# Edges in their own order, duplicates summed by an equality matrix, and sums kept in four DRAM tables

## The reference

```python
e = relu(edge_feat @ We1 + be1) @ We2 + be2          # 40000 x 256, hidden 512
msg = relu(node_feat[src] + e)
out_h = segment_sum(msg, dst, num_segments=2500)
out = relu(((1 + eps) * node_feat + out_h) @ Wn1 + bn1) @ Wn2 + bn2
```

## Time and profile before

| | us |
|---|---|
| median of 3 runs (3002.50 to 3002.54) | 3002.51 |
| span of the profiled execution | 3198.3 |
| TensorE busy in it | 2348.5 |
| VectorE busy | 1951.0 |
| POOL busy | 1194.9 |
| ScalarE busy | 1141.6 |

### The profile page before, as it was taken

The page is one execution under the profiler, slowest core; times in us unless marked ns, Lnnn a source line. Parts: engine busy times, 40 slices in busy tenths (PEclk is TensorE's granted clock), DMA queues, the critical chain, the costliest instruction groups (busy, mean ns, idle before and its releaser), DMA issues. The chain is left out here.

```text
span 3198.3 us, 54121 instructions
## 1 busy us (share of the span) xinstructions
PE 2348.5 (73%) x14408; PEld 1941.4 (61%) x14409; DVE 1951.0 (61%) x5493; ACT 1141.6 (36%) x2522; POOL 1194.9 (37%) x1158
## 2 busy tenths in 40 slices
PE   0994899999999999999743499997125556554676
PEld 0331788888888888888743388886124434443565
DVE  7997566666566666666683644444445555556773
ACT  0994334343343343434320155554011222212221
POOL 0001555555555555655000011111536676663000
PEclk9997899999999999999875699999567676766787
DMA  0001222222222222223100367675222233225000
GB/s 39 0 0 56 75 72 68 70 74 71 72 69 69 72 71 67 76 69 73 26 0 32 114 235 248 237 246 173 61 72 81 78 88 85 79 83 48 19 8 32
DMA packets 129241, 256.68 MB, mean 80 GB/s; under 512 B 26393, under 2 KB 64326, under 8 KB 128563
## 3 DMA queue, kind: packets, MB, share of 16 engines
q0 software_dynamic: 56480, 145.84, 17.1%
q1 hardware_dynamic: 72708, 110.19, 10.1%
HBM read 238.57 MB, written 17.34 MB: 80 GB/s over the span
## 5 line engine op out<-in xcount | busy, mean ns | idle before, releaser
L455 POOL DMA_INDIRECT edge_ea<-in_edge_attr_dram,edge_edge_idx x332 | 339.8, 1023 | 611.7 <-DVE edge_edge_idx L615 520.8
L578 ACT ACTIVATE edge_whole<-edge_h_ps,edge_b 128x512 f32<-128x512 f32 x332 | 227.3, 685 | 655.5 <-PE edge_h_ps L374 385.1
L1594 POOL DMA_INDIRECT att_got<-head_table,att_idx x352 | 372.0, 1057 | 225.3 <-issue 115.4
L461 POOL DMA_INDIRECT edge_nf<-node_table,edge_node_idx x332 | 359.4, 1082 | 221.0 <-DVE edge_node_idx L618 111.8
L373 PE MATMUL edge_e_ps<-edge_w_low,edge_hid_high 128*128 128x256 f32 x1328 | 375.0, 282 | 7.4 <-issue 7.3
L374 PE MATMUL edge_e_ps<-edge_w_high,edge_hid_high 128*128 128x256 f32 x1328 | 374.1, 282 | 8.3 <-issue 7.9
L372 PE MATMUL edge_e_ps<-edge_w_high,edge_hid_low 128*128 128x256 f32 x1328 | 375.3, 283 | 5.5 <-issue 5.1
L372 PE MATMUL edge_h_ps<-edge_eat_high,edge_w_low 128*128 128x512 f32 x664 | 280.1, 422 | 53.2 <-ACT edge_whole L578 45.6
L631 DVE TENSOR_TENSOR edge_hid_low<-edge_whole,edge_hid_high 128x512 fp32r<-128x512 f32 x332 | 231.8, 698 | 83.0 <-ACT edge_hid_high L583 42.6
L373 PE MATMUL edge_h_ps<-edge_eat_low,edge_w_high 128*128 128x512 f32 x664 | 276.5, 416 | 6.0 <-issue 6.0
L374 PE MATMUL edge_h_ps<-edge_eat_high,edge_w_high 128*128 128x512 f32 x664 | 275.7, 415 | 2.7 <-issue 2.5
(11 more groups left out here) (380 smaller groups left out, 5231.5 us busy)
## 6 DMA issues: line engine op xcount, KB each, us to landing
moe_w<-in_L_ffn_w_dram SPq DMA_DIRECT2D x162, 512.0 KB, 4.8
routed<-moe_out SPq DMA_DIRECT2D x54, 128.0 KB, 6.2
att_got<-head_table,att_idx POOLq DMA_INDIRECT x352
edge_ea<-in_edge_attr_dram,edge_edge_idx POOLq DMA_INDIRECT x332
edge_nf<-node_table,edge_node_idx POOLq DMA_INDIRECT x332
head_table<-hrow_rows SPq DMA_DIRECT2D x1, 2519.5 KB
x<-in_x_dram SPq DMA_DIRECT2D x1, 2500.0 KB
node_table<-edge_table_rows SPq DMA_DIRECT2D x1, 2500.0 KB
```

What stands on the lines that cost most here:

```text
L455: nc.gpsimd.indirect_dma_start(ea[u][:, j, :], None, io["edge_attr_256"][:, :], bass.IndirectOffsetOnAxis(ap=edge_idx[u][:, j:j + 1], axis ...
L461: nc.gpsimd.indirect_dma_start(nf[u][:, j, :], None, m.node_table[:, :], bass.IndirectOffsetOnAxis(ap=node_idx[u][:, j:j + 1], axis=0)).th ...
L578: act.activation(whole[c][:], h_ps[:, c % 2, :], ACT.Relu, bias=b1[:, c:c + 1]).then_inc(hid_whole, 1)
L1594: pool.indirect_dma_start(got[v][:, j, :], None, m.head_table[:, :], bass.IndirectOffsetOnAxis(ap=idx[v][:, j:j + 1], axis=0)).then_inc(la ...
```

## The change

The sort by dst and its placing are gone, with their tables. Edges are taken in their own order: group g is columns 4g to 4g+3 of the 125 x 320 layout, 80 groups of four blocks of 125 edges. SP loads them as plain rows of 4 KB (112 + 13 lanes, `SPLIT`) in place of POOL's gathers.

Edges of one block that share a dst are summed inside the block. `dst` is laid out by rows in DRAM (`dst_rows`, by three transposes on TensorE) and loaded for each group as `dst_row`, the same row for all 128 partitions. `find_same` compares it with each lane's dst: `same[p, q]` is 1 where edges p and q have one dst. `same` times the messages gives each edge the sum for its dst. The second form with `earlier` counts equal edges before it; `find_slots` sends edges with such a predecessor to a spare row (`move`), the others to row dst. ScalarE's `take_sums` copies the sums to `agg`, and POOL adds block j to table j in DRAM by an indirect DMA with `compute_op=ALU.add`. Each table's addition waits for that table's previous one. Table 0 starts with (1+eps) y, the others with zeros. `node_mlp` loads the four tables and adds them.

The loads of x and the biases move into `constants`, the layer norm into the head of `edge_messages`, between the splitting of the weights. The semaphores of the two stages are cleared and freed behind them.

```diff
+SUMS = 4
+EVEN = 112
+SPLIT = (slice(0, EVEN), slice(EVEN, LANES))
...
-    groups = EDGE_BLOCKS // G
-    tail = (groups - 3) // 2 * 2
+    groups = EDGE_COLS // G
+    N = G * LANES
+    tail = groups - 2
...
+                def load_edges(u, g):
+                    for lanes in SPLIT:
+                        sp.dma_start(ea[u][lanes], edges[lanes, bass.DynSlice(g * G, G), :]).then_inc(ea_landed[u], 16)
...
+                def refill(u, g):
+                    sp.wait_ge(turned, g - 1)
+                    load_edges(u, g)
+                    sp.wait_ge(repeats_found, g - 1)
+                    load_dst(u, g)
...
+                sp.wait_ge(own_ready, 1)
+                for lanes in SPLIT:
+                    sp.dma_start(m.sums[0][0:N_NODES, :].rearrange("(p t) d -> p t d", t=TILES)[lanes], own_rows[lanes]).then_inc(sums_begun, 16)
...
+                for k in range(1, SUMS):
+                    sp.dma_start(m.sums[k][0:N_NODES, :].rearrange("(p t) d -> p t d", t=TILES),
+                                 zeros[:].unsqueeze(1).to_broadcast([LANES, TILES, DIM])).then_inc(sums_begun, 16)
+                with sp.Fori(1, groups // 2) as turn:
+                    for u in range(2):
+                        refill(u, turn * 2 + u)
...
+                def next_nodes(g, u):
+                    pool.wait_ge(node_idx_ready, g + 1)
+                    pool.wait_ge(summed, g - 1)
+                    gather_nodes(u)
+
+                def add_sums(g, u, first=False):
+                    pool.wait_ge(slot_ready, g + 1)
+                    pool.wait_ge(agg_ready, g + 1)
+                    for j in range(G):
+                        k, n = j % SUMS, j // SUMS
+                        if not (first and n == 0):
+                            pool.wait_ge(sum_landed[k], g * (16 * G // SUMS) + 16 * n)
+                        own_waits(pool, m)
+                        pool.indirect_dma_start(m.sums[k][:, :], bass.IndirectOffsetOnAxis(ap=slot[u][:, j:j + 1], axis=0),
+                                                agg[u][:, j, :], None, compute_op=ALU.add).then_inc(sum_landed[k], 16)
...
+                next_nodes(2, 0)
+                pool.wait_ge(sums_begun, 32 + 16 * (2 * SUMS - 1))
+                add_sums(0, 0, first=True)
+                next_nodes(3, 1)
...
+            def take_sums(g, u, first=False):
+                act = nc.scalar
+                act.wait_ge(gathered, g + 2)
+                if not first:
+                    for k in range(SUMS):
+                        act.wait_ge(sum_landed[k], g * (16 * G // SUMS) - (16 * G // SUMS))
+                act.activation(agg[u][:], s_ps[0:LANES, :, :], ACT.Copy).then_inc(agg_ready, 1)
...
+                for j in range(G):
+                    last = nc.vector.scalar_tensor_tensor(before[:, j, :], dst_row[u][0:LANES, j * LANES:(j + 1) * LANES],
+                                                          dst[:, bass.DynSlice(g * G + j, 1)], m.earlier[:], ALU.is_equal, ALU.mult,
+                                                          accum_out=repeats[:, j:j + 1])
+                last.then_inc(repeats_found, 1)
...
+                        dve.wait_ge(sums_in[n // 2], SUMS * 32)
+                    if begun(n, 1):
+                        dve.wait_ge(z_ready, n)
+                    nc.vector.tensor_tensor(pair[0][:], sums[0][:, tiles, :], sums[1][:, tiles, :], ALU.add)
+                    nc.vector.tensor_tensor(pair[1][:], sums[2][:, tiles, :], sums[3][:, tiles, :], ALU.add).then_inc(pairs_ready, 1)
+                    dve.wait_ge(pairs_ready, n + 1)
+                    nc.vector.tensor_tensor(z[u][:], pair[0][:], pair[1][:], ALU.add).then_inc(z_ready, 1)
```

More of the change, by code:

```diff
@@ L402, in edge_messages @@
     msg_ready = sem("edge_msg_ready")
-    hot_ready = sem("edge_hot_ready")
-    scattered = sem("edge_scattered")
-    added = sem("edge_added")
+    same_ready = sem("edge_same_ready")
+    repeats_found = sem("edge_repeats_found")
+    moves_found = sem("edge_moves_found")
+    slot_ready = sem("edge_slot_ready")
+    gathered = sem("edge_gathered")
+    agg_ready = sem("edge_agg_ready")
+    sum_landed = [sem(f"edge_sum_landed{k}") for k in range(SUMS)]
     G = GROUP
-    groups = EDGE_BLOCKS // G
-    tail = (groups - 3) // 2 * 2
+    groups = EDGE_COLS // G
+    N = G * LANES
+    tail = groups - 2
     with ExitStack() as ctx:
@@ L411, in sb, with two @@
             return ctx.enter_context(nc.sbuf_tensor(f"edge_{n}", shape, dt))
+        def two(n, shape, dt=F32):
+            return [sb(f"{n}{u}", shape, dt) for u in range(2)]
         def parts(n, shape):
@@ L464, in _ @@
+                for k in range(SUMS):
+                    sp.wait_ge(sum_landed[k], groups * (G // SUMS) * 16)
             @block.gpsimd
             def _(pool):
[L466 to L473 removed]
@@ L495, in transposes @@
+                for u in range(2):
+                    add_sums(groups - 2 + u, u)
             def transposes(u, landed):
@@ L598, in act_group @@
                     eat_high(g + 1)
+                if first != 1:
+                    take_sums(g - 1, 1 - u, first=first in (2, 3))
             @block.scalar
@@ new lines, in find_slots @@
+            def find_slots(u, g, first=False):
+                cols = bass.DynSlice(g * G, G)
+                nc.vector.wait_ge(repeats_found, g + 1)
+                nc.vector.scalar_tensor_tensor(moves[:], repeats[:], 0.0, move[:, cols], ALU.is_gt, ALU.mult).then_inc(moves_found, 1)
+                nc.vector.wait_ge(moves_found, g + 2)
+                if not first:
+                    for k in range(SUMS):
+                        nc.vector.wait_ge(sum_landed[k], g * (16 * G // SUMS) - (16 * G // SUMS))
+                nc.vector.tensor_tensor(slot[u][:], moves[:], dst[:, cols], ALU.add).then_inc(slot_ready, 1)
@@ new lines, in _ @@
+                dve.wait_ge(high_split, 1)
+                nc.vector.tensor_tensor(w1l[:], w1[:], w1h[:].bitcast(F32), ALU.subtract).then_inc(weights_split, 1)
+                dve.wait_ge(gathered, 1)
+                for n, cut in enumerate(cuts):
+                    last = nc.vector.tensor_copy(dst_t[0:cut.stop - cut.start, n, :], s_ps[0:cut.stop - cut.start, n, 0:LANES])
+                last.then_inc(rows_made, 1)
+                dve.wait_ge(m.x_landed, 32)
+                for t in range(TILES):
+                    last = nc.vector.bn_stats(m.stats[:, t, :], m.x[:, t, :])
@@ new lines, in _ @@
+                chain.link(last)
+                for t in range(TILES):
+                    last = nc.vector.bn_aggr(mv[:, t, :], m.stats[:, t, :])
+                chain.link(last)
+                nc.vector.tensor_scalar(var[:], mv[:, :, 1], LN_EPS, None, ALU.add).then_inc(var_ready, 1)
+                dve.wait_ge(std_ready, 1)
+                chain.link(nc.vector.reciprocal(rstd[:], var[:]))
+                for t in range(TILES):
+                    last = nc.vector.tensor_scalar(m.y[:, t, :], m.x[:, t, :], mv[:, t, 0:1], rstd[:, t:t + 1], ALU.subtract, ALU.mult)
@@ L661, in _ @@
+                chain.link(last)
+                dve.wait_ge(m.rows_landed, 48)
                 nc.vector.tensor_tensor(table_rows[:], m.y[:], m.row_a[:, 0, :].unsqueeze(1).to_broadcast([LANES, TILES, DIM]),
[L662 to L665 removed]
+                                        ALU.add).then_inc(table_ready, 1)
@@ L666, in _ @@
+                dve.wait_ge(high_split, 2)
+                nc.vector.tensor_tensor(w2l[:], w2[:], w2h[:].bitcast(F32), ALU.subtract).then_inc(weights_split, 1)
                 eat_low(0)
-                nc.vector.memset(m.acc[:], 0.0).then_inc(zeroed, 1)
-                stage_edge_idx(0, 2)
-                def one_group(g, u, ahead=3, first=False):
+                chain.link(nc.vector.tensor_scalar(eps1[:], m.eps[:], 1.0, None, ALU.add))
+                nc.vector.tensor_scalar(own_rows[:], m.y[:], eps1[:, 0:1], None, ALU.mult).then_inc(own_ready, 1)
@@ L673, in one_group @@
+                def one_group(g, u, ahead=2, first=False):
                     add_nodes(1 - u, g - 1)
@@ L700, in _ @@
                 eat_low(1)
-                stage_edge_idx(1, 3)
-                one_hots(0, range(G))
-                dve.wait_ge(zeroed, 1)
+                find_same(0, 0, first=True)
+                find_slots(0, 0, first=True)
                 one_group(1, 1, first=True)
@@ L880, in node_mlp @@
         w2h, w2l = (sb(f"w2_{part}", [P, KH, DIM], F32R) for part in ("high", "low"))
-        eps1 = sb("eps1", [LANES, 1])
+        sums = [sb(f"sums{k}", [LANES, TILES, DIM]) for k in range(SUMS)]
+        pair = two("pair", [LANES, ST, DIM])
         z = two("z", [LANES, ST, DIM])
```

371 lines of the change are left out of this document (180 added, 191 removed).

## The result

| | kernel before | changed kernel |
|---|---|---|
| median, us | 3002.53 (3002.5 to 3003.15) | 3077.82 (3071.74 to 3082.28) |
| ratio of the changed kernel to before | | 1.0249, 95% interval 1.0234 to 1.0263 |
| span of the profiled execution, us | 3198.3; taken anew, 2998.8 | 3069.7 |

The changed kernel is 2.5% slower. The prediction was 2781 us and faster with 88%; its range, 2730 to 2900, missed.

A forecast was written before the change was run, and what follows sets the result against it. It took TensorE to bound the edge loop. Edge stage 255 us less and node stage 33 us more made 222 off the median 3002.5: 2781 us, by itself 2755 to 2820, with a range of 2730 to 2900 including rivals.

The forecast's parts named there:

- part 3: Edge loop: 80 groups at TensorE's 14.62 us profiled, 13.02 undisturbed; POOL covered at 11 us a group; end at 1308.
- The pauses: Edge loop of the profiled kernel before: pauses of about 5 us in some groups, 133 us, taken as mostly the profiling's.
- the 255: Edge stage: predicted to end at 1308 against 1563.6, 255 us less; 259 with the undisturbed steps.
- Part 1: Head: sort and placing go, layer norm stays; weights in at 21 us, VectorE's chain 54, TensorE's first product at about 48.
- Part 2: Filling of tables: three zero fills on five engines take 70 us, holding later edge loads and POOL's first addition.
- T: Time at which group 2's edges land and TensorE goes on: 140 us, from 127 to 152.
- Rival C: Table fills run on ten or sixteen engines, 22 to 35 us in place of 70: total 2733 to 2746; 11%.
- rival D: The 112-row transfers run on only five engines: 85 us more, total 2866; 6%.
- Rival B: Edge loop: POOL's issues bind at 1.9 us an addition, 14.3 us a group, or landing binds a little: 2881; 12%.
- Rival A: Edge loop: additions land late and become the bound, so the kernel is slower; 3327 at a 20 us landing; 9%.
- Part 4: Node stage: 33 us more, from weights 25 later behind four tables, node steps 6 and clearing semaphores 2.
- +0.7 a step: Node stage: z takes three additions for one, lengthening each step of 6.01 us by 0.7, 6 us in all.

The follow-up runs named there:

- before_again: The kernel before, unedited, profiled once more: 3000.67 us (one run), span 2998.8 us.
- fill16: The changed kernel with each of the three zero fills split into two transfers of 112 and 13 lanes: 3039.75 us.
- two_adds: The changed kernel with only the additions of blocks 0 and 1 of each group issued, leaving out half of the sums: 2834.26 us.
- plain_write: The changed kernel with a group's four scatters writing their rows in place of adding them: 2826.7 us.
- two_tables: The changed kernel with two tables, reordered POOL work, one split and earlier fill, node weights first, and the high-part copy in two-input form: 3141.71 us.

## Why the prediction was wrong, step by step

The miss is 3077.8 - 2781 = 297 us. In spans it is 293: the forecast was 222 less than before, and 70.9 more was measured (3069.7 - 2998.8). The step that failed is in part 3: the loop was taken for TensorE's, with POOL covered, and POOL is its bound. In the order of the prediction:

- **The pauses.** Held as reading (13.15 us a group undisturbed), but the sum was built on the paused trace. Its step "with 13.15 and 13.02 for the steps it is 259" also is a slip: by its own numbers it comes to 249. In before_again the node stage starts at 1421.9 and the predicted end of the edge stage, with 13.02 us steps, is 152.6 + 78 x 13.02 + 15.4 = 1183.6: 238 less. 17 us of the 255 were not there.
- **Part 1.** First product at 55.9 instead of 48. ScalarE waits for the weights until 29.7, where the sum has them in at 21 (its terms add up to 19, and it has none for the first two groups' edges, which SyncE loads right behind them), and VectorE starts on them at 30.8. own_rows takes 2.89 us, not 5.5. The sum of the chain, 54 for own_ready, came to 58.7.
- **Part 2.** Right in mechanism (five engines, SyncE's queue, POOL behind sums_begun) and 11 us short in size: T was 151.4 for 140, at the upper end of 127 to 152. The fills themselves took about the 70 us of the sum, from 74.3 to some 145; they began 8 us late, behind own_ready and the tails, and group 2's edges came 6 us after them. Rival C did not occur, but fill16 made it: 38 us against its 35 to 48. It also shows the 112-row pieces at a DMA share of 0.95, which rules out rival D.
- **Part 3.** The step that failed is "Covered while an addition costs under 1.6 us to issue", with the additions entered "at the gathers' price". They cost 2.15, and POOL 16.0 us a group for 11. Even the threshold was too high: with the gathers at the 1.24 us that they take here and TensorE's step at 12.91 it is (12.91 - 4 x 1.54) / 4 - 0.30 = 1.39 us. Rival B described this mechanism; it asked for 1.9 us and 14.3 a group, too little on both. two_adds prices it: 243 us. Against the 1183.6 above the node stage starts 244 us later: 9 at group 1's L745 (161.7 for 152.6), 228 in the 78 steps from there (15.94 us for 13.02), and 8 in the tail (23.1 for 15.4). The rest of part 3 held well: TensorE's own step 12.91 for 13.02, VectorE 732/78 = 9.4 us a group for 10.2, ScalarE 6.7 for 6.9, landing 6.4 us within the 4 to 12. In two_adds, where POOL is out of the way, the node stage starts at 1185.6, 2 us from the 1183.6; that it is so near is luck, since a start 9 us late and steps 0.11 us shorter cancel. Rival A did not hold, though its sign came: L773 waited for a landing 77 times. So this sign didn't tell A from B; L562's mean did.
- **Part 4.** 50 us for 33. From the start of the stage to its last output product on TensorE it takes 124.3 us for 73.9. The weights are 46 us later, not 25: at the 219 GB/s measured the 10.24 MB take some 47 us (an estimate), so the term "24 to 30 us" was mis-sized, beyond even the 16 us that the range allowed for it. "+0.7 a step" was not there: from first to last output product it takes 54.2 us for 53.9, so all of the 50 lie ahead of the first one.
- **The rest of the kernel**, entered at nothing, is 14.4 us longer (1517.4 for 1503.0). It is the attention stage, where POOL is full as well. The same gathers, in before_again and in the changed kernel:

```profile
L1594 POOL DMA_INDIRECT att_got<-head_table,att_idx x352 | 389.2, 1106 | 143.7 <-issue 107.0
```

```profile
L1684 POOL DMA_INDIRECT att_got<-head_table,att_idx x352 | 403.5, 1146 | 143.6 <-issue 107.0
```

403.5 - 389.2 is 14.3 us. Why a gather that the diff doesn't touch takes 40 ns more stays open; in plain_write it is 1117 ns, in two_adds 1158, in two_tables 1171.

Together 17 + (1428.0 - 1183.6 = 244) + 17 + 14 = 292 of the 293 us. The right bound was among the rivals, with 12% and too small a price: an operation that no row shows was given a gather's price, and the margin by its own threshold was 0.5 us on 1.08.

## What to carry to other kernels

Before an engine's instructions are exchanged for others of the same number, work out the price at which that engine becomes the bound, and ask how far the nearest row is from it. If no row shows the operation and 1.5 times the nearest one crosses the bound, the crossing is a main case and not a rival of 12%. And when a loop slows down, the longest wait names an engine that has time to spare, here VectorE, and not the bound; add up busy time and the gaps between instructions of each engine instead, here 1249 of 1254 us on POOL.

## What the runs showed of the hardware

- An indirect scatter of 125 rows of 1 KB takes POOL 1.20 us to issue (plain_write), a gather 1.24 in the changed kernel and 1.40 to 1.42 in two_adds and plain_write, and an accumulating scatter 1.96 at least, 2.15 on average in the changed kernel and 2.02 in two_adds. The queue shows 288 packets more for each accumulating one.
- An accumulating scatter lands 5.8 to 9.6 us after issue, median 6.4, in the changed kernel. With two tables, where a table's next one is issued 7.6 us later, POOL waited 2.5 us once a group.
- Three fills of 2.56 MB on 125 rows, 121 GB/s at a DMA share of 0.34, held SyncE at issue for 49 us; cut into 112 and 13 rows they held it for 31.3 us, at up to 291 GB/s.
- Reading back 10.24 MB as sixteen transfers, with 1.05 MB of weights behind them, took 51.5 us at 219 GB/s, the DMA engines 0.95 busy.
